# A gather loop on GpSimd: pacing by a cleared tile, replaced by a wait for the last transfer but one

## The reference

```python
edge_index = jnp.stack([src, dst])
h = jnp.maximum(_layernorm(x, axis=-1), 0.0)
x = x + _L0_gnn_ref(h, edge_weight, edge_attr_3, edge_index, w1, b1, w2, b2)
h = jnp.maximum(_layernorm(x, axis=-1), 0.0)
x = x + _L1_gnn_ref(h, edge_index, W1, b1, W2, b2, W3, b3)

def _L0_gnn_ref(features, abs_distances, rel_vec, edge_index, ...):
    R = relu(abs_distances[:, None] @ w1 + b1) @ w2 + b2      # 64 hidden, 384 radial values per edge
    Y = spherical_harmonics(rel_vec)
    Fj = features[src]                                         # gather of node rows
    ...                                                        # message of 32 values per edge
    return out.at[dst].add(msg)

def _gcn_conv(x, src, dst, norm, W, b, n_nodes):               # three times, with a relu behind each
    h = x @ W
    msg = h[src] * norm[:, None]                               # gather of node rows
    return segment_sum(msg, dst, n_nodes) + b
```

## Time and profile before

| | |
|---|---|
| median of 3 runs | 5776.53 us (5772.36 to 5779.69) |
| profiled execution, its time | 5779.69 us |
| its span, first to last instruction | 5779.7 us |
| POOL busy | 4889.1 us (85%) |
| PE, DVE, ACT busy | 4258.6, 3608.0, 2702.7 us (74%, 62%, 47%) |
| indirect transfers on POOL (L782) | 3616, 3636.6 us busy, 1006 ns each |
| clears on POOL (L762) | 3616, 1234.8 us busy, 341 ns each |

### The profile page before, as it was taken

One profiled execution on the slowest core, in us unless ns is written; L12 is line 12 of the kernel. 1 busy time (PEld: TensorE's weight loads), 2 busy tenths in 40 slices (PEclk: granted clock), 3 DMA queues, 4 the chain that ended last, 5 costly groups with the idle time before them and its releaser, 6 DMA issues.

```text
span 5779.7 us, 179150 instructions
## 1 busy us (share of the span) xinstructions
PE 4258.6 (74%) x62463; PEld 3147.7 (54%) x62464; DVE 3608.0 (62%) x8469; ACT 2702.7 (47%) x6550; POOL 4889.1 (85%) x7276
## 2 busy tenths in 40 slices
PE   5777777777777777755555555889898889766666
PEld 3444444444444444444444444778787778554554
DVE  8777777777777777776666666333333334555555
ACT  4444444444444444466666666344444444433333
POOL 7888888888888888768888888688888889588886
PEclk9999999999999999955555555899989999767767
DMA  3111111111111111333332332332333333444444
GB/s 87 33 33 33 33 33 31 33 33 33 33 33 32 32 33 33 36 71 77 77 77 77 77 77 71 114 90 85 91 91 85 91 91 100 119 119 126 122 127 107
DMA packets 494970, 400.88 MB, mean 69 GB/s; under 512 B 269575, under 2 KB 454828, under 8 KB 493537
## 3 DMA queue, kind: packets, MB, share of 16 engines
q10 hardware_dynamic: 146996, 207.67, 10.6%
q0 software_dynamic: 115712, 109.02, 10.3%
q1 hardware_dynamic: 231536, 74.48, 5.9%
HBM read 375.52 MB, written 15.29 MB: 68 GB/s over the span
## 4 chain that ended last, share of the span: by engine, by line
POOL 50%; issue 40%; PE 5%; POOLq 2%; DVE 2%; DMA 1%; ACT 0%; DVEq 0%; SPq 0%
POOL rows L782 29%; POOL pause L762 21%; POOLq L761 2%; PE radial L2067 2%; PE psX L2082 1%; PE psT L2082 1%; PE sums L2153 1%; PE radial L2209 0%; DMA table<-arena 0%; PE radial L2222 0%; DMA rows<-table,idx 0%; DMA xn<-in_x 0%; POOLq L760 0%; PE radial L2008 0%; DVE rows L1827 0%
## 5 line engine op out<-in xcount | busy, mean ns | idle before, releaser
L782 POOL DMA_INDIRECT rows<-table,idx x3616 | 3636.6, 1006 | 803.0 <-POOL pause L762 483.7
L762 POOL MEMSET pause<- 128x256 f32 x3616 | 1234.8, 341 | 2.5
L1942 PEld LDWEIGHTS sums<-scratch,onehot 128*64 128x64 f32 x9408 | 789.7, 144 | 465.0 <-DVE scratch L1377 228.6
L2067 PE MATMUL radial<-arena,shared 128*32 128x96 bf16 (+1 forms) x31200 | 926.4, 266 | 154.2 <-DVE shared L1613 75.1
L1942 PE MATMUL sums<-scratch,onehot 128*64 128x264 f32 (+1 forms) x9408 | 984.1, 356 | 32.6 <-DVE scratch L1377 26.2
L2067 PEld LDWEIGHTS radial<-arena,shared 128*32 128x32 bf16 (+1 forms) x31200 | 664.8, 116 | 294.4 <-issue 72.0
L2153 PE MATMUL sums<-onehot,rows 128*128 128x80 f32 (+1 forms) x2844 | 371.0, 298 | 576.7 <-DMA rows<-table,idx 571.8
L1007 ACT CAST scratch<-radial 128x480 bf16<-128x480 f32 x860 | 476.9, 555 | 665.7 <-PE radial L2067 657.6
L1360 DVE TENSOR_TENSOR scratch<-radial,shared 128x768 f32<-128x768 f32 x784 | 743.4, 948 | 0.0
L1927 PE MATMUL radial<-shared 64*128 64x384 f32 x3136 | 730.5, 546 | 0.0
L880 ACT COPY shared<-rows 128x192 f32<-128x192 f32 x196 | 89.4, 456 | 1264.1 <-DMA rows<-table,idx 1262.9
(11 more groups left out here) (237 smaller groups left out, 5969.3 us busy)
## 6 DMA issues: line engine op xcount, KB each, us to landing
scratch<-places_d ACTq DMA_DIRECT2D x242, 800.0 KB
rows<-table,idx POOLq DMA_INDIRECT x3616
shared<-in_edge_weight SPq DMA_DIRECT2D x390, 128.0 KB, 2.9
idx<-in_src SPq DMA_DIRECT2D x451, 4.0 KB
table<-arena SPq DMA_DIRECT2D x24, 256.0 KB, 2.8
table<-arena SPq DMA_DIRECT2D x2, 1176.0 KB, 10.6
accT<-in_edge_attr SPq DMA_DIRECT2D x2, 1152.0 KB
table<-arena SPq DMA_DIRECT2D x24, 96.0 KB, 2.0
```

Of the source, the lines that this page charges most:

```text
L762: nc.gpsimd.memset(pause[:, :], 0.0).then_inc(made, 1)
L782: (pool.indirect_dma_start(rows_3[:, r, j, :] if n in (1, 3) else rows[:, r, j, 0:WIDTH[n]], None, tables[n], bass.IndirectOffsetOnAxis(ap ...
L1942: last = nc.tensor.matmul(there, onehot[:, u % 2, 4 * h + t, 0:SW], taken_from, start=(h + q + part == 0), stop=(h == 1 and q == 1 and par ...
L2067: last = nc.tensor.matmul(d, from_src[n][:, h, i, t, :], table_of(n, s), start=True, stop=True, tile_position=(0, 32 * i))
```

## The change

The clear and its tile go. Ahead of each transfer POOL now waits until the last transfer but one has landed. For that, the four semaphores `gathered` (one for each buffer) become two, and the eight transfers of a group use them in turn. All who wait for a group now wait for both. The wait of transfer j for its predecessor on the same semaphore stands before transfer j; the clear stood behind it.

```diff
-PAUSE = 256
+IN_FLIGHT = 2
...
-        gathered = [sem(f"gathered{u}") for u in range(UNROLL)]
+        gathered = sems("gathered", IN_FLIGHT)
...
-        def rows_gathered(step, n, u, plus):
-            return step.times(step.groups // UNROLL * 16 * TPG, 16 * TPG * (rounds_before(n) + u // UNROLL + plus))
+        def rows_gathered(step, n, u):
+            each = 16 * TPG // IN_FLIGHT
+            return step.times(step.groups * each, each * (sum(GATHERED[:n]) + u + 1))
...
-                    sp.wait_ge(gathered[r], rows_gathered(step, n, u, 0))
+                    for landed in gathered:
+                        sp.wait_ge(landed, rows_gathered(step, n, u - UNROLL))
...
-            def pause_between(step, n, u, j):
+            def one_less_in_flight(step, n, u, j):
+                k = j % IN_FLIGHT
                 if step.peeled:
                     before = TPG * (sum(GATHERED[:n]) + step.it * step.groups + u) + j
-                    if before:
-                        pool.wait_ge(made, 9 + before)
+                    if before >= IN_FLIGHT:
+                        pool.wait_ge(gathered[k], before // IN_FLIGHT * 16)
                 else:
-                    pool.wait_ge(made, pool.snap(pauses))
-                    pool.reg_add(pauses, pauses, 1)
-                nc.gpsimd.memset(pause[:, :], 0.0).then_inc(made, 1)
+                    pool.wait_ge(gathered[k], pool.snap(in_flight[k]))
+                    pool.reg_add(in_flight[k], in_flight[k], 16)
...
                             col = j % 2 * KS + j // 2
+                            one_less_in_flight(step, n, u, j)
                             (pool.indirect_dma_start(rows_3[:, r, j, :] if n in (1, 3) else rows[:, r, j, 0:WIDTH[n]], None, tables[n],
                                                      bass.IndirectOffsetOnAxis(ap=idx[:, r, col:col + 1], axis=0))
-                                 .then_inc(gathered[r], 16))
-                            pause_between(step, n, u, j)
+                                 .then_inc(gathered[j % IN_FLIGHT], 16))
...
-                    act.wait_ge(gathered[u], rows_gathered(step, 0, u, 1))
+                    for landed in gathered:
+                        act.wait_ge(landed, rows_gathered(step, 0, u))
...
-                    pe.wait_ge(gathered[r], rows_gathered(step, n, u, 1))
+                    for landed in gathered:
+                        pe.wait_ge(landed, rows_gathered(step, n, u))
```

More of the change, by code:

```diff
@@ L61 @@
 PAD_REL = -1000.0
-PAUSE = 256
+IN_FLIGHT = 2
+assert TPG % IN_FLIGHT == 0
 assert NG % UNROLL == 0 and PTAIL * KS == ETAIL and PTAIL <= P and NG == 2 * NB
@@ L295, in gnn_kernel @@
         one = sb("one", [P, 1])
-        pause = sb("pause", [P, PAUSE])
         flag = sb("flag", [P, 1])
@@ L750, in _ @@
             turn = [pool.alloc_register(f"turn_pool{u}") for u in range(UNROLL)]
-            pauses = pool.alloc_register("pauses")
-            def pause_between(step, n, u, j):
+            in_flight = [pool.alloc_register(f"in_flight{k}") for k in range(IN_FLIGHT)]
+            def one_less_in_flight(step, n, u, j):
+                k = j % IN_FLIGHT
                 if step.peeled:
                     before = TPG * (sum(GATHERED[:n]) + step.it * step.groups + u) + j
-                    if before:
-                        pool.wait_ge(made, 9 + before)
-                else:
-                    pool.wait_ge(made, pool.snap(pauses))
-                    pool.reg_add(pauses, pauses, 1)
-                nc.gpsimd.memset(pause[:, :], 0.0).then_inc(made, 1)
+                    if before >= IN_FLIGHT:
+                        pool.wait_ge(gathered[k], before // IN_FLIGHT * 16)
+                else:
+                    pool.wait_ge(gathered[k], pool.snap(in_flight[k]))
+                    pool.reg_add(in_flight[k], in_flight[k], 16)
             def gathers(n):
@@ L806, in gathers @@
                     pool.reg_mov(turn[u], 2 * (LOOP[n][0] // UNROLL - 1) if n else 0)
-                pool.reg_mov(pauses, 9 + TPG * (sum(GATHERED[:n]) + LOOP[n][0]))
+                for k in range(IN_FLIGHT):
+                    pool.reg_mov(in_flight[k], 16 * TPG // IN_FLIGHT * (sum(GATHERED[:n]) + LOOP[n][0]))
                 sweep(pool, body, n)
```

## The result

The changed kernel takes 6773.35 us (median of 4 runs, 6762.73 to 6783.82) against 5774.61 us for the kernel before on the same occasions: 1.173 times as long, 95% interval 1.171 to 1.175. The prediction was 6490 us, with a range of 6110 to 6770. The direction held; the size was 280 us short, and the measured time lies just outside the range.

What follows compares the result with a forecast made beforehand. POOL's issuing of transfers was taken as the bound. The profiled 5779.7 us, plus 814 us for longer transfer periods, less 94 us for peeled transfers, gave 6500 us, stated as 6490 us; range 6110 to 6770.

Steps and rivals of the forecast that it cites:

- The bound: POOL sets the pace in 5520 of 5779.7 us, at 1.44 us per transfer, except in conv2's last step.
- W: Time from a landing to the start of the transfer that waited for it: 0.80 us, lower bound 0.18.
- The rival that the preparation stays hidden: The sequencer prepares the transfer and holds only its start, 0.18 us after landing: 5470 us in all; chance 0.08.
- the 608 peeled transfers: The wait belongs to the transfer itself; preparation ahead of it would give back 188 us, half taken: -94 us.
- L: Time from a transfer's start on POOL to its landing: 2.5, 2.65, 2.95, 3.0 us in layer 0, conv1, conv2, conv3.
- two transfers take L + W, and the period is (L + W) / 2: Period of POOL's transfers, while over 0.95 us of descriptors: 1.65, 1.725, 1.875, 1.90 us by layer; together +814 us.
- the 10.7 us of the accumulator's clear: Layer 0: POOL's clear between the first step and the loop, 10.7 us added to the stretch, then as now.
- the prediction's own sign: Layer 0 starts right (every second transfer 3.3 us apart) and total off over 200 us: miss lies in the convolutions' landing time.
- The rival "landings in the convolutions are longer": Landings of 3.5 us in conv2 and conv3 lengthen the periods by 0.275 and 0.25 us: 6840 us; chance 0.12.
- The rival "landings shorten": Less crowding brings landings to 2.32 us everywhere, period 1.56 us: 5810 us, or 6150 halfway; chance 0.12.

Runs made afterwards that it cites:

- three in flight: Changed kernel with each transfer waiting for the last but two, in place of the last but one; 5439.13 us, ratio 0.942 to the kernel before.
- four: Changed kernel with each transfer waiting for the last but three, in place of the last but one; 5072.58 us, ratio 0.878 to the kernel before.
- one chain of waits: Changed kernel with four semaphores: even transfers wait for the last but one, odd ones for the last but three; 6543.87 us, ratio 1.133 to the kernel before.
- one in flight: Changed kernel with each transfer waiting for the one before it, in place of the last but one; 12164.55 us (one run).

## Why the prediction came out as it did

**The bound** was right. Before, POOL's cadence set the time: without the clears a transfer takes 0.19 us less of spacing (1.25 for 1.44) and 0.04 us less of descriptors (967 for 1006 ns on the mean), which for 3616 transfers is 830 us, and the kernel became 857 us faster.

**W as a preparation** was right in the loops: 0.76 us in the chain of waits against 0.80 forecast, and the cause was the one named, a preparation that used to be hidden behind the clear. The rival that the preparation stays hidden is refuted for the loops. It holds in the 608 peeled transfers (0.26 us), of which I had taken half. By this the forecast was too high: 3008 x 0.04 / 2 = 60 us in the loops, and 608 x 0.54 / 2 = 164 us less the 94 taken, 70 us, in the peeled steps.

**L** was close: 2.50, 2.65, 2.95 and 3.00 us forecast, 2.51, 2.86, 2.93 and 3.06 us measured on the mean. Only conv1 was mis-sized (1.725 us a transfer forecast, 1.88 measured over 735 intervals). In all L was 93 us short, 76 of them in conv1. That conv2 and conv3 came out so near has luck in it: each value was read from one transfer in mid-layer, while single landings there lie between 2.3 and 6.2 us. The 0.05 to 0.15 us guessed for the consumer's own start is 0.02 us in the kernel before.

**The step that failed** is W in "two transfers take L + W, and the period is (L + W) / 2". The formula holds for each pair, if W is all the time from a landing to the start of the transfer that waited for it. The forecast put only the preparation into W and nothing for a transfer that is ready and stands behind another. But one POOL issues both chains in a fixed order, and a transfer whose own wait is over can't start before the one ahead of it, which may still wait. This is the 248 us above, and it is missing from the sum. Taking the second chain away gave a net 237 us back, and three in flight against four shows the same weakness of a sum over means from another side.

A second thing is missing from W. Inside the loops the sequencer now and then takes 3.20 us for the preparation that usually takes 0.48. The timeline of POOL in conv2 shows it together with a late landing:

```profile
5320.09 0.94 POOL L785 DMA_INDIRECT rows<-table,idx  x1 [0.96 <-DMA rows<-table,idx]
5322.87 0.94 POOL L785 DMA_INDIRECT rows<-table,idx  x1 [1.85 <-DMA rows<-table,idx]
5328.86 0.94 POOL L785 DMA_INDIRECT rows<-table,idx  x1 [5.04 <-issue]
5330.11 1.21 POOL L785 DMA_INDIRECT rows<-table,idx  x1 [0.30 <-issue]
```

and the chain of waits says what the third of them stood for:

```profile
5320.09 5.30 DMA rows<-table,idx
5325.39 0.02 issue
5325.41 0.03 POOLq L764
5325.44 3.20 issue
...
5328.86 2.59 DMA rows<-table,idx
```

The transfer of 5328.86 waited for the late landing at 5325.39 and then for the long preparation. The one behind it waited for the transfer of 5322.87, which had landed at 5325.55. It came 1.25 us after 5328.86, the shortest spacing that POOL has here: both chains paid for one long preparation. In layer 0 the changed kernel, one chain of waits and one in flight have 13 of them each, one in 109 to 113 transfers. Each makes both chains of the changed kernel 2.7 us late (35 us in layer 0). With one in flight it costs 2.7 us once, 1.35 in the half, and with one chain of waits some 1.4 us. So it is a part of the differences above, some 18 us in layer 0. Before, 1.40 us of such a pause showed at a time. Why it comes is open.

Together: the preparation was 130 us over-estimated, L was 93 us short, and the standing behind others with the rest of W (long preparations, and the instructions at a group's head) took 328 us, of which the sum had only the 10.7 us of the accumulator's clear. That makes the miss: forecast stretches 6334 - 94 = 6240 us, measured 6522, 282 us between them. Without the over-estimate of the preparation it would have been over 400. By the prediction's own sign (starts of every second transfer in layer 0 right, 3.37 us against 3.3, and a total off by over 200 us) the miss would be L in the convolutions; L there has 83 us of it.

The rival "landings in the convolutions are longer" is nearest in time (6840 us), but not by its mechanism: it had L at 3.5 us in conv2 and conv3, and 2.93 and 3.06 were measured. The rival "landings shorten" failed: even alone they are not at 2.32 us on the mean.

**What stays open.** Late landings in the convolutions go with the loads of `scratch<-places_d`, and layer 0 has none of these. No run takes these loads away, so this is a coincidence in time, seen in two traces, and not an experiment. The transfers far from a load also land 0.06 us later with two in flight in layer 0 and 0.10 to 0.11 us later in the convolutions; no run says why. The larger rows of conv2 (512 B) are not the main reason for the longer landings with company: the growth from one to two in flight is smallest there among the convolutions (0.19 us, against 0.25 and 0.37 with rows of 192 B).

## What to carry to other kernels

In the loops here, where the wait was an instruction of its own with a register addition behind it, it moved the sequencer's preparation of the transfer behind the wait (0.76 us); as part of the transfer's own instruction it did not (0.26 us). Read such a price where the engine stood idle ahead of an instruction of that kind, not where a neighbour covered it. With a limit on transfers in flight, don't sum over mean landings: the late ones count, in-order issue makes each chain pay for the other, and a delay that hits all transfers under way is not halved by having two. One or two more in flight were worth more than the whole change here (6773 us with two, 5439 with three, 5073 with four). Before replacing one means of pacing by another, run the kernel with neither.

## What was not expected of the hardware

Behind a clear a transfer starts after 0.16 us, behind another transfer after 0.30 us (the earlier trace rows and the timelines above). So a clear of 0.33 us cost 0.33 + 0.16 - 0.30 = 0.19 us per transfer, not its whole length. And single transfers of 128 rows take up to 6.2 us to land in the convolutions, some 2.5 times their usual time. From the changed kernel's chain of waits, one each in conv1, conv2 and conv3, and below them the loads of ACT's queue that were issued at the same time:

```profile
2928.50 5.95 DMA rows<-table,idx
...
4997.97 6.20 DMA rows<-table,idx
...
6075.40 6.18 DMA rows<-table,idx
```

```profile
2928.46 0.42 ACTq L972 DMA_DIRECT2D scratch<-places_d  x1
...
4997.64 0.38 ACTq L972 DMA_DIRECT2D scratch<-places_d  x1
...
6075.19 0.38 ACTq L972 DMA_DIRECT2D scratch<-places_d  x1
```
